# Four tiles to a target window in the aggregation stages of a graph network: one PSUM sum, one add and one-hots in fours

## The reference

```python
# appnp: twice (hop1, hop2), with self loops
msg = norm[:, None] * x[src];  agg = segment_sum(msg, dst);  x = 0.5 * agg + 0.5 * h
# hyperedges: the targets below 2500 are the hyperedges
d_v = segment_sum(hyperedge_weight[he_idx], node_idx)          # he_idx = dst, node_idx = src
he_feat = segment_sum(x_prime[node_idx], he_idx)               # stage "hyperedges"
out = segment_sum(he_feat[he_idx], node_idx)                   # stage "members"
# light: weighted by an edge's own weight, over rows = src
side = segment_sum(vals[:, None] * emb[cols], rows)            # stage "light"
# attention over edges with a softmax over all of them           stage "attend"
```

## Time and profile before

| | |
|---|---|
| median of 3 runs | 9374.24 us (9363.55 to 9376.87) |
| span of the profiled execution | 9384.6 us (no other time of it is on record) |
| instructions | 117794 |
| PE, PEld busy | 3786.3 us (40%), 3178.0 us (34%) |
| DVE busy | 4076.7 us (43%) |
| ACT busy | 1279.6 us (14%) |
| POOL busy | 5152.0 us (55%) |
| gathers of the five stages | 3696, 959 ns each |
| DMA | 520.79 MB, 666914 packets, mean 55 GB/s |

### The profile page before, as it was taken

The page is one execution under the profiler, slowest core; times in us unless marked ns, Lnnn a source line. Parts: engine busy times, 40 slices in busy tenths (PEclk is TensorE's granted clock), DMA queues, the critical chain, the costliest instruction groups (busy, mean ns, idle before and its releaser), DMA issues. The chain is left out here.

```text
span 9384.6 us, 117794 instructions
## 1 busy us (share of the span) xinstructions
PE 3786.3 (40%) x17207; PEld 3178.0 (34%) x17208; DVE 4076.7 (43%) x16680; ACT 1279.6 (14%) x5244; POOL 5152.0 (55%) x5326
## 2 busy tenths in 40 slices
PE   6333333333343333222333333333333335666665
PEld 3222222233333333212332223232333225555654
DVE  8444444544443222123333333343333355555656
ACT  0000000000000000020001111110000024444443
POOL 0555555466666666635665666655666625555551
PEclk5555555555555555565555555555555557888886
DMA  9111111111111111101112323221111123333332
GB/s 151 50 37 37 37 37 36 43 44 43 44 44 43 44 44 44 43 22 51 45 44 58 66 65 66 65 49 51 45 44 44 44 47 91 93 90 91 95 92 44
DMA packets 666914, 520.79 MB, mean 55 GB/s; under 512 B 516265, under 2 KB 566836, under 8 KB 666628
## 3 DMA queue, kind: packets, MB, share of 16 engines
q0 software_dynamic: 183232, 378.81, 16.0%
q1 hardware_dynamic: 483380, 139.33, 7.6%
q10 hardware_dynamic: 144, 1.28, 0.0%
HBM read 439.09 MB, written 79.95 MB: 55 GB/s over the span
## 5 line engine op out<-in xcount | busy, mean ns | idle before, releaser
L386 POOL DMA_INDIRECT gathered<-node_table,idx x3696 | 3544.3, 959 | 2686.2 <-ACT idx L376 1350.2
L400 PE MATMUL ps<-onehots,gathered 128*128 128x128 f32 x7392 | 2097.7, 452 | 3883.7 <-issue 1946.2
L400 PEld LDWEIGHTS ps<-onehots,gathered 128*128 128x128 f32 x7392 | 1722.9, 313 | 4259.1 <-issue 3711.5
L460 DVE TENSOR_TENSOR agg<-agg,ps 128x128 f32 x3696 | 1063.4, 288 | 2736.5 <-PE ps L400 986.9
L936 POOL DMA_INDIRECT gathered<-node_table_xq,idx x832 | 794.7, 955 | 815.3 <-PE ps L1037 306.8
L630 POOL DMA_INDIRECT bucketed_edges<-edge_rows,idx x782 | 777.4, 994 | 428.1 <-issue 261.2
L448 DVE TENSOR_SCALAR onehots<-iota,off_now 128x128 f32<-128x128 f32 x2880 | 688.6, 300 | 54.2 <-issue 33.1
L679 PE MATMUL ps<-gathered 128*128 128x49 f32 x1568 | 346.3, 414 | 655.0 <-DVE gathered L664 468.2
L679 PEld LDWEIGHTS ps<-gathered 128*128 128x128 f32 x1568 | 338.2, 332 | 663.1 <-DVE gathered L664 473.2
L376 ACT CAST idx<-src_t 128x4 int32 x516 | 99.8, 193 | 3255.7 <-PE ps L400 2221.6
L1025 PE MATMUL ps<-Wh,eT 128*128 128x128 f32 x1664 | 406.3, 332 | 51.7 <-issue 47.6
(11 more groups left out here) (257 smaller groups left out, 4262.6 us busy)
## 6 DMA issues: line engine op xcount, KB each, us to landing
gathered<-node_table,idx POOLq DMA_INDIRECT x3696
bucketed_edges<-edge_rows SPq DMA_DIRECT2D x52, 544.0 KB
edge_rows<-bucketed_edges SPq DMA_DIRECT2D x204, 136.0 KB
edge_rows<-bucketed_edges SPq DMA_DIRECT2D x208, 128.0 KB
edge_rows<-in_edge_attr_dram SPq DMA_DIRECT2D x192, 128.0 KB
gathered<-node_table_xq,idx POOLq DMA_INDIRECT x832
bucketed_edges<-edge_rows,idx POOLq DMA_INDIRECT x782
node_table<-t_nodes SPq DMA_DIRECT2D x3, 3136.0 KB
```

The costliest lines, as they stand in the source:

```text
L386: nc.gpsimd.indirect_dma_start(g[:, k, :], None, table, bass.IndirectOffsetOnAxis(m.idx[:, k:k + 1], 0)).then_inc(S["landed"][k], 16)
L400: nc.tensor.matmul(m.ps[:, k % 8, 0:P], g[:, k, :], m.oh[:, k % 8, :], start=True, stop=True).then_inc(S["used"], 1)
L460: V.tensor_tensor(w, w, m.ps[:, k % 8, 0:P], ALU.add).then_inc(S["added"], 1)
```

## The change

In the three stages in order of `dst`, the four tiles of a quarter share one window. `prepare` finds for each group of four tiles its lowest and its highest target (`gstart`, `glast`), for which it makes 14 rounds of diagonal, matmul and reduction in place of 7 rounds with a copy. PE sums the four matmuls in one PSUM bank, and DVE adds once a quarter. In members and light the four matmuls go into column slices of one bank, and the 16 adds stay.

There are now 16 one-hot slots; DVE makes the one-hots of all four quarters and then does the adds. An unweighted quarter is one tensor_tensor of 128x512 with both operands broadcast. In light a weighted one-hot is still one instruction a tile, but reads its offset and weight in place, at an address from a register, where they were copied to a fixed place before. PE waits for one-hots and PSUM once a quarter.

`HyperedgeWeights` picks with one 128x512 multiply and one reduction a quarter. `members` loads no rows any more: the three numbers of every edge (12 bytes out of a row of 272) are fetched by SP with four DMAs during the hyperedges, into `m.side`, and the windows stage spreads them with two copies and a subtraction.

```diff
-            for c in range(CH):
+            for n in range(2 * CH):
+                c, top = n // 2, n % 2
...
+                V.tensor_scalar(m.oh[:, n % 2, :], m.ident[:, :], (m.tmin, m.tmax)[top][:, c:c + 1], None, ALU.mult).then_inc(S["diag"], 1)
+                v.wait_ge(S["replicated"], n + 1)
+                four = m.ps[:, n % 4, 0:w].rearrange("p (t g) -> p t g", g=G)
+                V.tensor_reduce((m.gstart, m.glast)[top][:, c * (P // G):c * (P // G) + w // G], four, AX.X,
+                                (ALU.min, ALU.max)[top]).then_inc(S["rep_used"], 1)
...
-        if load_rows:
+        if meta is not None:
             @block.sync
             def _(sp):
...
-                with sp.Fori(0, I) as i:
-                    for q in range(4):
-                        hold(sp, S["rows_read"][q], i + 1)
-                        sp.dma_start(m.erow[:, 4 * q:4 * q + 4, :],
-                                     a.bucketed[bass.ds((i * U + 4 * q) * P, 4 * P), :].rearrange("(t p) d -> p t d", p=P)).then_inc(S["rows"][q], 16)
+                for k in range(META):
+                    t0, n = k * (BT // META), BT // META
+                    sp.dma_start(meta[:, t0:t0 + n, :],
+                                 a.bucketed[t0 * P:(t0 + n) * P, DE:DE + 3].rearrange("(t p) d -> p t d", p=P)).then_inc(S["meta"], 16)
+                sp.wait_ge(S["meta"], 16 * META)
...
                 for k in range(U):
-                    pe.wait_ge(S["onehot"], nt + k + 1)
+                    q, e = k // G, k % G
+                    if e == 0:
+                        pe.wait_ge(S["onehot"], n * NQ + q + 1)
+                        if dst_order:
+                            pe.wait_ge(S["added"], n * NQ + q + 1)
+                        else:
+                            pe.wait_ge(S["added"], nt + G * q + G)
                     pe.wait_ge(S["landed"][k], nt + 16)
-
-                    pe.wait_ge(S["added"], nt + k + 1)
-                    nc.tensor.matmul(m.ps[:, k % 8, 0:P], g[:, k, :], m.oh[:, k % 8, :], start=True, stop=True).then_inc(S["used"], 1)
+                    if dst_order:
+                        nc.tensor.matmul(m.ps[:, q, 0:P], g[:, k, :], m.oh[:, k, :], start=e == 0, stop=e == G - 1).then_inc(S["used"], 1)
+                    else:
+                        nc.tensor.matmul(m.ps[:, q, e * P:(e + 1) * P], g[:, k, :], m.oh[:, k, :], start=True, stop=True).then_inc(S["used"], 1)
...
+                for q in range(NQ):
+
+                    v.wait_ge(S["used"], nt + G * q + G)
+                    here = m.oh[:, G * q:G * q + G, :]
+                    if weight is None:
+                        V.tensor_tensor(here, m.iota[:, :].unsqueeze(1).to_broadcast([P, G, P]),
+                                        off[:, bass.ds(t0 + G * q, G)].unsqueeze(2).to_broadcast([P, G, P]), ALU.is_equal).then_inc(S["onehot"], 1)
+                    else:
+                        for e in range(G):
+                            k = bass.ds(t0 + G * q + e, 1)
+                            last = V.tensor_scalar(m.oh[:, G * q + e, :], m.iota[:, :], off[:, k], weight[:, k], ALU.is_equal, ALU.mult)
+                        last.then_inc(S["onehot"], 1)
                     if side:
-                        side.quarter(v, nt, q, S)
...
-                onehots(0)
-                onehots(1)
-                adds(0)
-                onehots(2)
-                adds(1)
-                onehots(3)
-                adds(2)
-                adds(3)
...
+        V.tensor_tensor(m.junk[:, :, :], m.oh[:, G * q:G * q + G, :],
+                        m.side[:, bass.ds(start, WIN)].unsqueeze(1).to_broadcast([P, G, WIN]), ALU.mult).then_inc(S["picked"], 1)
+        v.wait_ge(S["picked"], n * 2 * NQ + 2 * q + 1)
+        V.tensor_reduce(m.picked[:, G * q:G * q + G], m.junk[:, :, :], AX.X, ALU.add).then_inc(S["picked"], 1)
...
-            step(V.memset(m.dst[:, :], 0.0))
-            step(V.memset(m.off[:, :], -1.0))
+            step(V.memset(m.dst[:, BT:], 0.0))
+            step(V.tensor_copy(m.ew[:, :], m.meta[:, :, 0]))
+            step(V.tensor_copy(m.dst[:, 0:BT], m.meta[:, :, 1]))
+            step(V.tensor_tensor(m.off[:, :], m.meta[:, :, 2], m.start[:, :], ALU.subtract))
```

More of the change, by code:

```diff
@@ L298, in _, with aggregate @@
             T.matmul(m.ps[:, 7, 0:NB], m.zerob[:, :], m.zerob[:, 0:NB], start=False, stop=True).then_inc(S["hist_used"], 1)
-def aggregate(nc, m, a, name, table, idx, dst_order, iters, weight=None, side=None, last_he=False, load_rows=False):
-    off = m.off
+def aggregate(nc, m, a, name, table, idx, dst_order, iters, weight=None, side=None, last_he=False, meta=None):
+    off, NQ = m.off, U // G
     g = m.gather[:, 0:U * D].rearrange("p (t d) -> p t d", d=D)
[L310 to L315, removed]
-            n = eng.value_load(m.smallI[0:1, 0:1], min_val=1, max_val=NB + 1)
-            return n
+    with phase(nc, name, f"landed*{U} idx_ready used onehot added round dve side picked reg meta") as (S, block):
         def iterations(eng):
@@ L455, in adds @@
-                def adds(q):
-                    v.wait_ge(S["used"], nt + 4 * q + 4 + U)
-                    for k in range(4 * q, 4 * q + 4):
-                        v.wait_ge(S["added"], nt + k + 8)
-                        w = m.agg[:, bass.ds(start[k], WIN)]
-                        V.tensor_tensor(w, w, m.ps[:, k % 8, 0:P], ALU.add).then_inc(S["added"], 1)
-                onehots(0)
-                onehots(1)
-                adds(0)
-                onehots(2)
-                adds(1)
@@ L466, in body @@
-                onehots(3)
-                adds(2)
-                adds(3)
+                if dst_order:
+                    start = window_starts(nc, mybir.EngineType.DVE, m, i * NQ, NQ)
+                else:
+                    start = window_starts(nc, mybir.EngineType.DVE, m, t0, U)
+                for q in range(NQ):
+                    v.wait_ge(S["used"], nt + G * q + G)
[8 more added lines that the diff above has]
+                        last.then_inc(S["onehot"], 1)
+                    if side:
+                        side.quarter(v, n, q, start[q], S)
@@ new lines, in body @@
+                for q in range(NQ):
+                    v.wait_ge(S["used"], nt + G * q + G + U)
+                    if dst_order:
+                        v.wait_ge(S["added"], n * NQ + q + a0)
+                        w = m.agg[:, bass.ds(start[q], WIN)]
+                        V.tensor_tensor(w, w, m.ps[:, q, 0:P], ALU.add).then_inc(S["added"], 1)
+                        continue
+                    for e in range(G):
+                        v.wait_ge(S["added"], nt + G * q + e + a0)
+                        w = m.agg[:, bass.ds(start[G * q + e], WIN)]
+                        V.tensor_tensor(w, w, m.ps[:, q, e * P:(e + 1) * P], ALU.add).then_inc(S["added"], 1)
@@ L511, in before, with quarter @@
         step(self.nc.vector.memset(self.m.rank[:, :], 0.0))
-    def quarter(self, v, nt, q, S):
-        pass
-    def tile(self, v, nt, k, start, o, S):
+    def quarter(self, v, n, q, start, S):
         pass
```

151 lines of the change are left out of this document (54 added, 97 removed).

## The result

The changed kernel takes 9097.7 us (median of 4 runs, 9092.7 to 9104.0) where the kernel before takes 9375.6 on the same chip: a ratio of 0.9704, 95% interval 0.969 to 0.9718. That is 278 us less; I had said 8830 us, 542 less. The sign and the range hold, the size is half. The experiments, on other chips, then showed that the sign is not the same on every chip.

A forecast was written before the change was run, and what follows sets the result against it. POOL's gathers, at least 20.0 us a pass, plus POOL's waits bound the kernel. Savings 306 + 82 + (66 - 15) + 151 - 36 - 10 - 2 = 542 us give 8830 us; own range 8550 to 9050, 8-in-10 range 8400 to 9220.

The forecast's parts named there:

- the rival in which the crawl stays: Aggregate stages: something other than instruction count starts the crawl, so only hop1 gains, 201 us less 12; 9185 us, chance 0.20.
- the crawl: PE or DVE, late in a pass while gathers are issued: each instruction slows, on PE 1.05 us against 0.12.
- What bounds the kernel: Five aggregate stages: POOL's 16 gathers need at least 20.0 us a pass; its waits, 1122.6 us, are the most to win.
- DVE there is itself the longest cycle: Hop1, before the change: DVE crawls and sets the 28.1 us pass; afterwards 15.6 to 19.8 us, under POOL's 20.0.
- The PE step: Aggregate stages: 42 PE instructions for 66 make PE's pass 19.7 us, with 1.0 us a pass left for the crawl.
- Hop1: Hop1 stage: of 414.0 us of waits all but 2.2 us a pass go, 306 us saved.
- Members, hop2 and hyperedges: These stages' waits fall to 1.6 us a pass: 151, 82 and 66 us saved, the last less 15 for loads.
- Light: Light stage: 30 more DVE instructions cost 0.7 us a pass, 36 us lost; bounds 200 gained and 220 lost.
- The loads of 12 bytes: Hyperedges: four DMAs of 106,496 pieces hold SP's queue about 190 us; 15 us charged for sharing DMA engines with gathers.
- Prepare: Prepare stage: 14 rounds of diagonal, matmul and reduction in place of 7 cost 10 us.
- The port: Aggregate stages: DVE compares or multiplies with two SBUF inputs delay POOL 0.15 us each, 0.6 us a pass, 1.2 in hop1.
- the rival at 9360 us: Aggregate stages: each compare stops POOL for its full 0.73 us, losing 527 us, so time stays as before; chance 0.03.

The follow-up runs named there:

- chip B: Chip of the fifth to seventh runs; kernel before and changed kernel, both run as they are: 7802.4 and 7849.8 us, ratio 1.0063.
- the first experiment: Changed kernel, but PE's matmuls signal `used` once a quarter instead of once a tile: 7850.5 us, 1.0054 to the kernel before.

## Why the prediction came out as it did

*The range.* My forecast had a range of its own, 8550 to 9050 us, and 9098 lies outside it. It lies within 8400 to 9220 because that range also holds the rival in which the crawl stays. So the mechanism that I had put first did not come true.

*What bounds the kernel.* Right for POOL and its 20.0 us a pass: without the hold every stage but hop2 stands at 20.0 to 21 us. "DVE there is itself the longest cycle" was right of the trace I had, and an effect of the hold, not of DVE's work: 20.1 us a pass on chip B with the same 118 instructions.

*The PE step.* "Leave 1.0 us a pass for what is left of the crawl" is the term that was mis-sized. Going by the waits for ACT, 749 us stayed where my sum leaves 1122.6 - 306 - 82 - 66 - 151 = 518 (light unchanged). In the hyperedges PE went from 66 to 42 instructions and DVE from 75 to 32, and the pass from 23.7 to 23.0 us. I had priced each slow instruction of PE at 1.05 us and made their sum the length of the pass. The slow ones did go, further than I had said: PE's sequencer has 254 instructions of over 300 ns in the hyperedges before and 67 after, in members 422 and 1. But the pass did not follow. PE's register instruction in light, before and after:

```profile
L399 PEldq FUSED_REGOPS  x808: 3/37/1061, 6374.5 to 7582.2; - x162
L383 PEldq FUSED_REGOPS  x804: 37/37/37, 6049.1 to 7303.3; - x161
```

None is slow any more, and POOL's waits for ACT rose there from 200 to 241 us. So the step that failed is that PE's slow instructions set the pass. In the hyperedges the time is lost in signals that arrive up to 11 us late, in light ahead of DVE's one-hots. The rival "the crawl does not go by the count" had hop1 alone gaining, 9185 us; the result lies 87 us from that and 268 from my forecast. The rival was the better description, and hop1's 230 of the 278 us say so. Shorter loops did hardly better (23.0 us a pass in the hyperedges for 23.7, with 24 instructions less on PE and 43 less on DVE), and no run here shows what holds the signals back.

*Hop1.* 230 us less, predicted 306. The order of the terms was right. That it came from DVE's pass, which lost half of its instructions, fits the rows but was not tested under a hold. Its compare and multiply take 0.69 us as estimated, its reduction 0.69 and not 0.57.

*Members, hop2 and hyperedges.* 31, 33 and 21 us, predicted 151, 82 and 51: the same term as PE's step. *Light.* 49 us more, predicted 36. *The loads of 12 bytes*: in the sum as 15 us, and not to be seen. The 190 us on SP's queue were wrong too. SP, changed kernel:

```profile
3985.50 57.26 SPq L338 DMA_DIRECT2D side_rows<-bucketed_edges  x4
```

It issues for 57 us, and the DMA engines, 90% busy or more in nearly all of this time, are through with these pieces by 4064, 78 us after the start. So the pieces of 12 bytes took less than half of the time that I had carried over from those of 272. *Prepare*: +7, predicted +10.

*The port.* Predicted 0.6 us a pass and 1.2 in hop1; measured without a hold 0.2 and 0.8 (39.1 us in 49 passes). "The port" is my name for what a DVE operation with two SBUF inputs adds to a gather beside it; that the second input costs it is shown by iota's move to PSUM (gathers of 959 ns on B, 946 with the move, in the hyperedges). Had each compare stopped POOL for its whole length, as in the rival at 9360 us, four would have cost 2.9 us a pass, by my estimate of 0.73 for one. The scan comes near to that: the gather that met it took 2.32 us against 0.94, 1.38 more, where 1.57 of the scan's 1.85 were left. The compares do not: of four in a row one gather pays 0.37 us, the second nothing. No run shows why.

*What I had not on the list*: that the profile of before was taken on a chip where 1570 of its 9375 us are the hold. It is not a matter of the five stages alone: they have 1054 us of it (5750 for 4696 on B), the bucket stage with its scatters 171 (1188.5 for 1017.5), and what follows light 343 (1801 for 1458). The change takes waits away there and adds port time and prepare's 8 us, and where nothing waits only what it adds is left: -3.0% on that chip, +0.6% on chip B. No rival of mine had this.

## What to carry to other kernels

When an engine idles with "issue" or its plain register instructions take ten times their usual time and more in part of a loop (a median of 690 ns for 50 on PE), that can be a sign, as it was here, that something outside the program sets the pace; run the unchanged kernel once more, on another chip, before a change is designed against it. Where POOL issues gathers back to back, DVE operations beside it with two SBUF inputs lengthened gathers (959 ns for 946 with the compares in the hyperedges, 2.32 us for 0.94 beside the scan); put a constant operand (iota, ones) into a free PSUM column, which cost nothing that shows here and gave 0.5% (iota, changed kernel) and 0.7% (ones, kernel before) where nothing was held.

## What the hardware showed that I had not expected

The same program takes 7800 us on some chips and 9375 on others, with the runs on one chip within 0.5% of each other. On the slower ones PE's signals were seen to reach others up to 11 us late while gathers are issued (in hop1 of the kernel before it is DVE that idles); neither fewer instructions, nor a quarter of the signals, nor twice the gather buffers lifts the pace above some 16 tiles in 23 us. What does this stays open. One rival nobody tested: that the recording has a part in it. Of the updates that hop1's 784 tiles make to `used`, the trace of the kernel before has 562 on the chip of the result and 778 on B, so records of the trace are lost where the hold is; and no time here comes from a run without a recorded span.

TensorE's granted clock in hop1 was 1.00 in the changed kernel and 0.52 before, and on B, where hop1 of the changed kernel also had 1.00, POOL set the pace all the same. In four runs of the first experiment the mean clock was 0.584 once and about 0.67 three times, and the one at 0.584 was the fastest, 7840.8 us.
